# Projection weights loaded and split by column thirds, and a chunk's transposes made in two visits

## The reference

```python
xn = layernorm(x)                                  # eps 1e-5, no scale or shift
q, k, v = split(xn @ W_qkv, 3)                     # W_qkv is 512 x 1536; 16 heads of 32
attn = softmax(q @ k.T / sqrt(32) + alibi_bias + causal_mask)
y = (attn @ v) merged over heads, @ W_o
logits = xn @ wg                                   # 8 experts
probs = softmax(logits); idx = argmax(probs); gate = probs[idx]
ffn = gate * (xn @ W[idx].T + b[idx])              # top-1 expert of each token
out = x + y + ffn
```

## Time and profile before

| | |
|---|---|
| three executions | 1753.88, 1759.58, 1758.34 us, median 1758.34 |
| profiled execution | 1754.4 us |
| its span | 1752.7 us |
| TensorE busy | 1626.1 us, 93% |
| VectorE busy | 1044.3 us, 60% |
| ScalarE busy | 750.1 us, 43% |
| GpSimd busy | 876.1 us, 50% |
| granted TensorE clock, mean | 0.962 of full |

### The profile page before, as it was taken

How to read it: one execution, slowest core, us unless ns; L and a number is a source line. 1 busy time by engine, 2 the same in 40 slices (tenths; PEclk the granted TensorE clock), 3 DMA queues, 4 the chain that set the end, 5 groups by cost and what they waited for, 6 DMA issues and landing times. The chain is left out here.

```text
span 1752.7 us, 26965 instructions
## 1 busy us (share of the span) xinstructions
PE 1626.1 (93%) x9266; PEld 988.5 (56%) x9267; DVE 1044.3 (60%) x2452; ACT 750.1 (43%) x1575; POOL 876.1 (50%) x869
## 2 busy tenths in 40 slices
PE   5999999689599999999999999999999997799898
PEld 4777777544254554554554554554554433588686
DVE  6434332487576776776776776776776700544366
ACT  2222222114354555565555555555555564411110
POOL 4500000006776676676676676676676676223360
PEclk8999999859899999999999999999999998899899
DMA  6655554592901901901901901901900400455595
GB/s 225 222 175 187 179 190 170 151 163 51 163 11 31 172 8 27 176 8 30 173 9 27 176 8 27 177 8 26 177 9 28 184 7 24 164 154 163 197 396 222
DMA packets 98236, 205.68 MB, mean 117 GB/s; under 512 B 11180, under 2 KB 28620, under 8 KB 92476
## 3 DMA queue, kind: packets, MB, share of 16 engines
q1 hardware_dynamic: 84200, 172.26, 38.6%
q0 software_dynamic: 9248, 23.53, 4.3%
q10 hardware_dynamic: 4672, 8.41, 1.7%
HBM read 124.55 MB, written 79.07 MB: 116 GB/s over the span
## 5 line engine op out<-in xcount | busy, mean ns | idle before, releaser
L1115 ACT ACTIVATE probs_sb<-score_ps 128x512 f32<-128x512 f32 (+3 forms) x1280 | 585.0, 552 | 475.8 <-PE score_ps L1187 451.1
L1017 DVE TENSOR_REDUCE part_max<-max_ps 128x1 f32<-128x512 f32 x768 | 473.4, 679 | 211.9 <-PE max_ps L1155 209.9
L1155 PE MATMUL max_ps<-k_aug,q_aug 104*128 104x512 f32 (+3 forms) x1280 | 508.9, 410 | 54.6 <-DMA k_aug<-steps_d 37.4
L1187 PE MATMUL score_ps<-q_aug,k_aug 106*128 106x512 f32 (+4 forms) x1280 | 478.8, 396 | 8.7 <-ACT probs_sb L1115 7.3
L964 POOL TENSOR_TENSOR quad_sum<-probs_sb 128x512 f32<-128x512 f32 x288 | 360.0, 1285 | 164.3 <-ACT probs_sb L1115 141.0
L1155 PEld LDWEIGHTS max_ps<-k_aug,q_aug 104*128 104x128 f32 x1280 | 247.0, 194 | 241.6 <-DVE part_max L1017 86.7
L1187 PEld LDWEIGHTS score_ps<-q_aug,k_aug 106*128 106x128 f32 (+1 forms) x1280 | 241.0, 189 | 145.6 <-ACT probs_sb L1115 122.8
L1231 PE MATMUL acc_ps<-probs_sb,v_sb 128*32 128x512 f32 (+3 forms) x2560 | 291.2, 541 | 0.0
L1013 DVE CUSTOM_DVE_ANT_0 max_ps<-max_ps,mask_row 128x384 f32<-128x384 f32 (+3 forms) x512 | 239.2, 515 | 69.1 <-PE max_ps L1155 68.1
L971 POOL TENSOR_TENSOR quad_sum<-quad_sum,probs_sb 128x512 f32<-128x512 f32 x192 | 239.2, 1283 | 0.0
L980 POOL TENSOR_SCALAR_AFFINE_SELECT probs_sb<-probs_sb 128x512 f32<-128x512 f32 x128 | 80.3, 636 | 207.9 <-ACT probs_sb L1115 207.4
(11 more groups left out here) (177 smaller groups left out, 1753.6 us busy)
## 6 DMA issues: line engine op xcount, KB each, us to landing
k_aug<-k_hi_d SPq DMA_DIRECT2D x14, 1024.0 KB
q_aug<-q_hi_d SPq DMA_DIRECT2D x14, 1024.0 KB
slot_y_d<-y_rows SPq DMA_DIRECT2D x39, 256.0 KB, 2.0
xn_d<-xn SPq DMA_DIRECT2D x8, 1024.0 KB, 5.3
q_hi_d<-st_hi SPq DMA_DIRECT2D x32, 256.0 KB, 3.5
q_lo_d<-st_lo SPq DMA_DIRECT2D x32, 256.0 KB, 3.6
k_hi_d<-st_hi SPq DMA_DIRECT2D x32, 256.0 KB, 2.5
k_lo_d<-st_lo SPq DMA_DIRECT2D x32, 256.0 KB, 2.9
```

Source lines behind the costliest of these rows:

```text
L1017: nc.vector.tensor_reduce(part_max[:, hh * QT + i, kc:kc + 1], max_ps[:, bank, 0:w], AX.X, ALU.max).then_inc(max_taken, 1)
L1115: nc.scalar.activation(probs[:, r % P_SLOTS, hh, off:CH], score_ps[:, (r * HG + hh) % S_BANKS, off:CH], ACT.Exp).then_inc(exp_done, 1)
L1155: nc.tensor.matmul(max_ps[:, bank, 0:w], q_aug[0:ROW_MAX, half, hh, i * P:(i + 1) * P], k_aug[0:ROW_MAX, half, hh, kc * CH:kc * CH + w], s ...
L1187: nc.tensor.matmul(score_ps[:, u % S_BANKS, off:CH], k_aug[rows, half, hh, jb * P:(jb + 1) * P], q_aug[rows, half, hh, cc * CH + off:(cc + ...
```

## The change

The weight matrix is handled in thirds of its columns (q, k, v) instead of blocks of rows. SP loads third 0, then the second chunk of x, then thirds 1 and 2, with the router's weights ahead of them all. ACT and DVE split third 0 before the first chunk, third 1 inside chunk 0 before product group 2's evacuation, third 2 before group 5's. TensorE waits for third 0 before chunk 0, for third 1 before group 4 and for third 2 before group 8.

Apart from that, the transposes of the next chunk, with their high and low parts, are made in two visits: blocks 0 and 1 before group 5, blocks 2 and 3 before group 6.

```diff
--- before.py
+++ after.py
@@ -268,7 +268,9 @@
     BANKS = 4
-    AHEAD = 6
+    TURN_AT = {5: (0, 1), 6: (2, 3)}
+    THIRDS = 3
+    SPLIT_AT = {2: 1, 5: 2}
     NV = 12
@@ -364,7 +366,7 @@
         v_stored = [sem("v_stored0"), sem("v_stored1")]
-        w_loaded, wg_loaded = [sem(f"w_loaded{k}") for k in range(KC)], sem("wg_loaded")
+        w_loaded, wg_loaded = [sem(f"w_loaded{t}") for t in range(THIRDS)], sem("wg_loaded")
         w_hi_done, w_lo_done, wg_done = sem("w_hi_done"), sem("w_lo_done"), sem("wg_done")
@@ -374,6 +376,10 @@
+        def is_first(ch):
+            return isinstance(ch, int) and ch == 0
@@ -392,11 +398,12 @@
                     sp.dma_start(xt[:, 0, a], x_c[0][:, a]).then_inc(x_loaded[0] if a == TPC - 1 else x_first[a], 16)
-                for k in range(KC):
-                    sp.dma_start(w_f[:, k], m.w_qkv[k * P:(k + 1) * P, :]).then_inc(w_loaded[k], 16)
-                    if k == 0:
-                        sp.dma_start(wg_f[:], m.w_g.rearrange("(k p) n -> p k n", p=P)).then_inc(wg_loaded, 16)
-                sp.dma_start(xt[:, 1], x_c[1]).then_inc(x_loaded[1], 16)
+                sp.dma_start(wg_f[:], m.w_g.rearrange("(k p) n -> p k n", p=P)).then_inc(wg_loaded, 16)
+                w_k = m.w_qkv.rearrange("(k p) n -> p k n", p=P)
+                for t in range(THIRDS):
+                    sp.dma_start(w_f[:, :, t * D:(t + 1) * D], w_k[:, :, t * D:(t + 1) * D]).then_inc(w_loaded[t], 16)
+                    if t == 0:
+                        sp.dma_start(xt[:, 1], x_c[1]).then_inc(x_loaded[1], 16)
@@ -554,8 +561,14 @@
-                def low_parts(ch, half):
-                    for k in range(KC):
+                def low_weights(t):
+                    dve.wait_ge(w_hi_done, t + 1)
+                    here = slice(t * D, (t + 1) * D)
+                    nc.vector.tensor_tensor(w_lo[:, :, here], w_f[:, :, here], w_hi[:, :, here].bitcast(F32), ALU.subtract).then_inc(
+                        w_lo_done, 1)
+                def low_parts(ch, half, tiles=range(KC)):
+                    for k in tiles:
                         dve.wait_ge(tr_hi_done, ch * KC + k + 1)
@@ -654,8 +667,10 @@
                     for e in range(NQK):
-                        if e == AHEAD and more:
-                            low_parts(ch + 1, 1 - half)
+                        if e in TURN_AT and more:
+                            low_parts(ch + 1, 1 - half, TURN_AT[e])
+                        if is_first(ch) and e in SPLIT_AT:
+                            low_weights(SPLIT_AT[e])
                         if not more:
@@ -676,9 +691,7 @@
                                         ALU.subtract).then_inc(wg_done, 1)
-                for k in range(KC):
-                    dve.wait_ge(w_hi_done, k + 1)
-                    nc.vector.tensor_tensor(w_lo[:, k], w_f[:, k], w_hi[:, k].bitcast(F32), ALU.subtract).then_inc(w_lo_done, 1)
+                low_weights(0)
                 chunk_pairs(dve, body)
@@ -688,8 +701,13 @@
-                def high_parts(ch, half):
-                    for k in range(KC):
+                def high_weights(t):
+                    act.wait_ge(w_loaded[t], 16)
+                    here = slice(t * D, (t + 1) * D)
+                    nc.scalar.activation(w_hi[:, :, here], w_f[:, :, here], ACT.Copy).then_inc(w_hi_done, 1)
+                def high_parts(ch, half, tiles=range(KC)):
+                    for k in tiles:
                         act.wait_ge(transposed, ch * KC + k + 1)
@@ -701,8 +719,10 @@
                     for e in range(NQK):
-                        if e == AHEAD and more:
-                            high_parts(ch + 1, 1 - half)
+                        if e in TURN_AT and more:
+                            high_parts(ch + 1, 1 - half, TURN_AT[e])
+                        if is_first(ch) and e in SPLIT_AT:
+                            high_weights(SPLIT_AT[e])
                         if not more and e == 3:
@@ -718,16 +738,14 @@
                 high_parts(0, 0)
-                for k in range(KC):
-                    act.wait_ge(w_loaded[k], 16)
-                    nc.scalar.activation(w_hi[:, k], w_f[:, k], ACT.Copy).then_inc(w_hi_done, 1)
+                high_weights(0)
                 chunk_pairs(act, body)
...
             def _(pe):
-                def transposes(ch, half):
+                def transposes(ch, half, tiles=range(KC)):
                     pe.wait_ge(xn_done, (ch + 1) * TPC)
-                    for k in range(KC):
+                    for k in tiles:
@@ -745,8 +763,11 @@
                     for n in range(NG):
-                        if n == AHEAD and more:
-                            transposes(ch + 1, 1 - half)
+                        if n in TURN_AT and more:
+                            transposes(ch + 1, 1 - half, TURN_AT[n])
+                        if is_first(ch) and n in (NQK // 2, NQK):
+                            pe.wait_ge(w_lo_done, 2 if n < NQK else THIRDS)
                         if n == 1 and not more:
@@ -779,7 +800,7 @@
                 pe.wait_ge(wg_done, 3)
-                pe.wait_ge(w_lo_done, KC)
+                pe.wait_ge(w_lo_done, 1)
                 chunk_pairs(pe, body)
```

## The result

The changed kernel took 1743.71, 1739.99, 1737.86 and 1739.03 us, median 1739.5, against 1756.1 for the kernel before on the same chip: ratio 0.990, 95% interval 0.988 to 0.992. The forecast of 1746.7 had started from a median of 1758.3, so 2.2 of the 7.2 us between it and 1739.5 are the starting point. In a second measurement the ratio was 0.9925 (0.9906 to 0.9944).

The account below looks back on a forecast made before the run. The prediction took TensorE's work and gaps to bound the projection stage. 4.0 us at the start plus 7.6 for the visits made 11.6 us, 1742.8 off the profiled execution and 1746.7 off the median; range 1740 to 1753.

Parts of the forecast that it names:

- What bounds the stage: Projection stage: lasts as long as TensorE's work and its gaps, 8.9 us before the first product and 8.0 in transposes.
- carried to the end: End of the stage: its last stores, routing tail and next loads all shift along with TensorE, so nothing keeps its old time.
- The start: Opening of the stage: splitting only third 0 first lets TensorE begin the router at 21.15 instead of 25.18, 4.0 us earlier.
- The cost of the slow clock: First matmuls of the stage: TensorE starts at 1.2 GHz, which costs 2.1 us; this cost is kept and only moved.
- The splits in chunk 0: Thirds 1 and 2 split inside chunk 0: hidden, with slack 0.46 us before group 4 and 4.4 us before group 8.
- The visits: Transposes of the next chunk in two visits: the 1.17 us wait goes, 1.09 us a chunk, 7.6 us in 7 chunks.
- The bounds of 7.0 to 8.2: Range of the visits' gain: 7.0 us with 0.1 more a visit, 8.2 with no cost of the change to matmuls.
- the largest gain: Likeliest case's best end: 5.0 + 8.2 = 13.2 us with the clock giving 2.1 back, 1739 us.
- Late splits: Rival in chunk 0: pieces take half as long again, third 1 is 1.6 us late; 1750.4 us, chance 0.08.
- a wait that stays: Rival: the second visit still waits for `xT_lo` as long as before; 4.0 us gained only, 1754.3 us, chance 0.04.
- a gain absorbed: Rival at the boundary to the next stage: something not tied to TensorE absorbs the gain; 1758 us, chance 0.04.
- the clock decides something: Rival in the next stage: TensorE's low clock ends later after the shift, making the kernel slower, 1767.7 us; chance 0.03.

Follow-up runs that it names:

- experiment 2: The changed kernel with all four blocks turned in one visit before group 6 again, weights still in thirds; ratio 0.9991 to the kernel before.
- experiment 9: The changed kernel with TensorE's first wait for the low weights put behind the eight router products; median 1735.9 us, ratio 0.990 to the kernel before.

## Why the prediction was wrong

- **What bounds the stage: right.** TensorE's work and its gaps, and nothing else; both gaps went as the change meant them to, and what was gained in the stage was carried to the end.
- **The start, 4.0 us: right in size.** Both durations came out to 0.01 us. Against the first profile the router began only 2.7 us earlier, since that profile had an early norm; against the second it is 4.1 (26.55 to 22.48). Counted from the first transpose, the router began after 13.15 and 13.36 us before the change and after 9.15 and 9.33 with it: 4.0 less, the quicker compared with the quicker and the slower with the slower. The cost of the slow clock was rightly kept: 6 and 10 slow steps in the two profiles of the change, 9 in both of before.
- **The splits in chunk 0: right.** From the end of third 1's low part to group 4 it was 0.65 us where the working had 0.56 (5.60 - 5.04); neither group 4 nor group 8 waits.
- **The visits, 7.6 us: the step that failed.** The mechanism was right, the term was mis-sized: 10.8 us. That eight transposes "take 1.01 us at their own pace (48.10 to 49.11)" was false. That stretch held the fourth block's wait of 0.18 us; their own pace is 0.79. By it the second half could have started at 46.71, not 46.93, so the wait ahead of it was 1.39 and not 1.17. Two times 0.79 instead of 3.19 us, less 0.07 for one more change of instruction, is the 1.54 that was measured. The bounds of 7.0 to 8.2 took the same row for their ends, and so held no error of the row itself. 3.2 us of the 5.0 missed are this term.
- **The rest,** some 1.8 us, is nothing that the profiles show: their stage ends give 14.4 us, and the repeated measurement 13.6 between the medians. The first measurement's interval goes from 14.2 to 20.7 us by the ratio, so 14.4 is inside it, at its edge; where the other 2.2 us of its 16.6 come from is not shown.
- **The range.** Its lower end was not the one that was worked out: the largest gain gave 1739, and the range was stated from 1740. That 1739 would have held the 1739.5 is luck: it counted on 2.1 us given back by the clock at the start, where by the slow steps of its two profiles the change got back 0.6 and lost 0.2.
- **The rivals.** Late splits, a wait that stays and a gain absorbed are all refuted for this kernel. That the clock decides something was a rival in the wrong place. In the next stage it did nothing that could be told from chance, but together with the longer wait that brought it down it took what the thirds alone could give (experiment 2). The prediction priced the two edits as a plain sum, and they are not one: 10.8 for the visits by the chunks, between nothing and 2.1 us for the thirds by themselves, by the stage ends of two profiles on either side (339.07 and 338.23 against 339.04 and 340.29), and 14.4 for both. With third 2 split one group earlier (337.10) the thirds by themselves gave 1.9 to 3.2. The visits take away the wait that the third's split would have made longer.

The Trainium skill, "TensorE: Matmul & The Clock Gate", Part 1, says that the number of slow matmuls differs between runs of one kernel. The runs agree: 6 and 10 in two profiles of the change, none and 11 in the two of the kernel of experiment 9.

## What to carry to other kernels

A gap of TensorE is to be read on its weight loads as well as on its matmuls, and the pace of an operation from a stretch in which nothing waits; a merged row of a count can hold a wait. A piece of work moved into the shade of another is free only if nothing that TensorE waits for stands behind it on its engine: a wait made 1.2 us longer cost as much again through the clock. One profile of before is one draw: its opening was 1.1 us early, and the part that no edit touched differed by 4 us between two profiles of one kernel.

## What was not expected of the hardware

- TensorE's granted clock fell in the midst of work: behind a wait of 2.3 us between transposes (two profiles of two), and behind 32 transposes of 16 columns that kept it busy for 2.1 us without a gap (two profiles of twelve; four or five matmuls at full pace stood in between, and the same transposes had no slow step behind them in the other ten, so this cause is not shown). Each time 4 to 8 matmul steps of 0.43 us followed, instead of 0.23.
- The clock column read 1.00 from 22 to 26 us in the first profile of the changed kernel and 0.50 in the second, while the steps were 0.43 us in both: the pace of starts shows the level where the column does not.
- With 1.7 us between the opening transposes and the router the first matmuls ran at full pace once (19.44 to 20.82, 0.23 a step), though the first eight transposes had taken about twice as long as later ones (1.94 us, against 1.03). Its second eight took 1.81 us, and 1.97 in the repeat, whose router was slow: the two profiles of that kernel differed already before the router. Short second eights (1.75 to 1.81 us) stand in three other profiles too, where the router came 4.9 or 8.9 us after the transposes and was slow all the same. With 4.9 us or more between them the start was always slow.
